# Image pipeline with stages moved between the attention pairs, a second pair of slack, and one residual addition moved from VectorE to GpSimd

## The reference, cut to what matters

```python
block 0:  x = x + _L0_conv_ref(_gn(x), ...)   # 16 images, 128 x 32 x 32, fp32
    shared = silu(group_norm(conv1x1_grouped(x)))            # 8 groups
    two experts of 8, chosen per image by a router:
    expert_out = sum_k rw[k] * silu(group_norm(conv3x3_grouped(x, expert k)))
    return shared + expert_out
block 1:  x = x + _L1_conv_ref(_gn(x), ...)                  # _gn: 32 groups
    qkv = qkv_w @ x + qkv_b;  windows of 8x8 pixels, 8 heads of 16 channels
    attn = softmax(q @ k.T / 4 + bias);  o = attn @ v
    out = proj_w @ (o + depthwise_conv7x7(v)) + proj_b
```

## Time and profile before

| | us |
|---|---|
| median of 3 runs | 931.92 |
| lowest and highest | 928.15, 932.22 |
| the profiled execution | 934.59 |
| its span, first to last instruction | 932.9 |
| its mean granted TensorE clock | 0.879 of full |

### The profile page before, as it was taken

One profiled execution on the slowest core, in us unless ns is written; L12 is line 12 of the kernel. 1 busy time (PEld: TensorE's weight loads), 2 busy tenths in 40 slices (PEclk: granted clock), 3 DMA queues, 4 the chain that ended last, 5 costly groups with the idle time before them and its releaser, 6 DMA issues.

```text
span 932.9 us, 18414 instructions
## 1 busy us (share of the span) xinstructions
PE 743.6 (80%) x6926; PEld 422.7 (45%) x6926; DVE 578.1 (62%) x1136; ACT 457.7 (49%) x746; POOL 197.0 (21%) x289
## 2 busy tenths in 40 slices
PE   6143768888888989888989887979797989978785
PEld 5121334454545554545454545454545456534321
DVE  4724456675767666767676757575757587632296
ACT  1204546555555564646464646464646465344422
POOL 3122123131213140403130313131313020000044
PEclk9976969797979797979888988888988989999999
DMA  9224444545464545455554545454546254586435
GB/s 353 106 71 116 139 113 146 145 128 156 144 178 136 163 148 150 150 153 165 142 170 128 173 136 173 123 173 120 177 132 177 67 176 132 161 276 217 156 157 203
DMA packets 84046, 145.29 MB, mean 156 GB/s; under 512 B 24179, under 2 KB 48886, under 8 KB 83958
## 3 DMA queue, kind: packets, MB, share of 16 engines
q1 hardware_dynamic: 58102, 100.89, 34.8%
q0 software_dynamic: 21248, 25.36, 10.9%
q10 hardware_dynamic: 4608, 17.86, 5.2%
HBM read 84.21 MB, written 51.41 MB: 145 GB/s over the span
## 4 chain that ended last, share of the span: by engine, by line
PE 41%; DMA 19%; DVE 16%; ACT 8%; issue 7%; SPq 6%; POOL 1%; POOLq 1%; ACTq 0%; DVEq 0%
PE g L1061 11%; DMA sk_d<-khl 10%; PE g L1057 5%; PE g L1079 4%; PE t L1127 4%; DMA stack<-sk_d 3%; SPq L298 3%; ACT xw L540 3%; PE s L1116 3%; PE pv L1142 3%; DMA vt<-x 3%; PE t L1241 2%; PE s L1112 2%; SPq L292 2%; PE s L1241 2%
## 5 line engine op out<-in xcount | busy, mean ns | idle before, releaser
L806 DVE BATCH_NORM_STATS2 st<-y 128x6 f32<-128x512 f32 x96 | 66.6, 694 | 147.6 <-ACT y L522 147.6
L522 ACT ACTIVATE y<-g 128x512 f32<-128x512 f32 x96 | 57.2, 596 | 167.0 <-PE g L1061 87.0
L1061 PE MATMUL g<-xsh,wsel 96*128 96x512 f32 x256 | 127.8, 627 | 14.0 <-DMA xsh<-xs 10.5
L595 ACT ACTIVATE pt<-t 128x512 f32<-128x512 f32 x128 | 76.2, 597 | 118.8 <-PE t L1127 112.2
L870 DVE TENSOR_REDUCE mx<-s 128x8 f32<-128x512 f32 x128 | 87.8, 686 | 69.6 <-PE s L1116 69.6
L1127 PE MATMUL t<-ident,less 128*128 128x128 f32 x512 | 97.6, 321 | 3.7 <-DVE less L874 3.7
L1142 PE MATMUL pv<-vp,pt 128*64 128x34 f32 x2048 | 95.2, 242 | 5.0 <-ACT pt L595 4.8
L1112 PE MATMUL s<-bias,ident 128*128 128x512 f16 x128 | 56.7, 443 | 52.9 <-DMA stack<-sk_d 52.8
L1142 PEld LDWEIGHTS pv<-vp,pt 128*64 128x64 f32 x2048 | 80.1, 154 | 31.4 <-issue 25.0
L874 DVE TENSOR_TENSOR less<-s,mx 128x512 f32<-128x512 f32 x128 | 88.5, 692 | 4.4
L1079 PE MATMUL g<-xw,w 128*128 128x512 f32 x128 | 66.7, 640 | 15.4 <-ACT y L522 11.7
(11 more groups left out here) (159 smaller groups left out, 1158.5 us busy)
## 6 DMA issues: line engine op xcount, KB each, us to landing
xsh<-xs POOLq DMA_DIRECT2D x64, 210.0 KB, 5.4
stack<-sq_d SPq DMA_DIRECT2D x96, 128.0 KB, 3.1
stack<-sk_d SPq DMA_DIRECT2D x192, 64.0 KB, 2.8
xs<-xn ACTq DMA_DIRECT2D x16, 578.0 KB, 2.9
vt<-x SPq DMA_DIRECT2D x4, 2048.0 KB, 17.7
xin<-x POOLq DMA_DIRECT2D x16, 512.0 KB, 5.8
acc_d<-xr SPq DMA_DIRECT2D x16, 512.0 KB, 5.5
sq_d<-qhl SPq DMA_DIRECT2D x16, 512.0 KB, 7.7
```

The costliest lines, as they stand in the source:

```text
L522: act.activation(y[:, k, h * HALF:(h + 1) * HALF], g[h][:, :], ACT.Identity).then_inc(g_free[h], 1)
L595: act.activation(pt[:, p % 2].rearrange("p i w n -> p (i w n)"), tbk[p % 2][:, :], ACT.Exp).then_inc(sem["exp_done"], 1)
L806: last = v.bn_stats(st[:, 2 * k + h, :], y[:, k, h * HALF:(h + 1) * HALF])
L1061: last = mm(g[h][:, :], wsel[:, k - 1, C * dy:C * dy + C], xsh[:, k - 1, dy + 16 * h:dy + 16 * h + 16, 0:W], start=(dy == 0), stop=(dy == 1))
```

## The change

The stages are put in other pairs, PE gets scores two pairs ahead, `pt` gets a third place, the halves of q and k are saved each by itself, the `g` banks are used in one alternating order for both halves, and `residual` part 0 becomes `add_input` on POOL, between `choose_affine` and the `rsqrt` of x; `split_v` stays last in POOL's turn and its DMAs are issued by SP in the turn after. No arithmetic changes. The waits on `g_ready` and `g_free` take their bank and count from the new order (`wait_ready`, `wait_emptied`).

```diff
     for b in range(B + 1):
+        use("y2", b + 2, (0,))
+        use("q", b + 1, (0,))
+        use("y2", b + 2, (1,))
+        use("q", b + 1, (1,))
+        use("k", b + 1)
+        use("v", b + 1)
+        use("ot", b - 1, (1,))
+        use("pr", b - 1)
+        use("vt", b + 1)
+        use("y0", b + 3)
+        use("y1", b + 3)
+        use("ot", b, (0,))
+    return {key: (n % 2, n // 2) for n, key in enumerate(order)}
...
-        pt = sb("pt", [C, 2, Q, 2, TOK])
+        pt = sb("pt", [C, 3, Q, 2, TOK])
...
+            def save_half(j, half, name, dst, src, saved):
+                cols = slice(HALF * half, HALF * half + HALF)
+                wait_emptied(sp, name, j, half)
+                if j:
+                    sp.wait_ge(stacked[half], STACK * j)
+                sp.dma_start(dst.rearrange("t c n -> c t n")[:, :, cols], src[:, :, cols]).then_inc(saved[half], 16)
...
             def step(b, has1, has2, has3):
+                if b:
+                    load_x1(b - 1)
                 place_v(b)
                 if has1:
                     save_q(b + 1)
                     save_k(b + 1)
-                    stack_qk(b + 1, 0)
+                    stack_q(b + 1, 0)
+                    stack_k(b + 1, 0)
                 if b:
                     save_acc(b - 1)
-                load_x1(b)
                 if has1:
-                    stack_qk(b + 1, 1)
+                    stack_q(b + 1, 1)
+                    stack_k(b + 1, 1)
                 if has2:
                     save_xr(b + 2)
...
+            def add_input(j):
+                pool.wait_ge(sem["silu_done"], 3 * j + 1)
+                if j:
+                    pool.wait_ge(sem["xr_saved"], 16 * j)
+                    pool.wait_ge(sem["xw_done"], j)
+                nc.gpsimd.tensor_tensor(xr[:, :], y[:, 0, :], xin[:, j % 2, :], ALU.add).then_inc(sem["sum_shared"], 1)
...
             def step(b, has1, has2, has3):
                 if has3:
-                    load_x(b + 3)
-                if has1:
-                    rsqrt(b + 1, 1, 1)
-                if has3:
                     load_rows(b + 3)
                 if has2:
                     rsqrt(b + 2, 0, 3)
                 if has3:
                     choose_affine(b + 3)
+                if has2:
+                    add_input(b + 2)
+                if b + 4 < B:
+                    load_x(b + 4)
+                if has2:
+                    rsqrt(b + 2, 1, 1)
                 if has1:
                     split_v(b + 1)
```

More of the change, by code:

```diff
@@ L357, in _ @@
             save_k(0)
-            stack_qk(0, 0)
-            stack_qk(0, 1)
+            for half in range(2):
+                stack_q(0, half)
+                stack_k(0, half)
             save_xr(1)
             images(step)
+            for c in range(TAP_RING):
+                load_taps(c)
+            load_x1(B - 1)
             save_acc(B - 1)
@@ L467, in _ @@
             choose_affine(2)
+            add_input(1)
+            load_x(3)
+            rsqrt(1, 1, 1)
             images(step)
@@ L574, in vt_out @@
                                                   ACT.Identity)
-                    last.then_inc(g_free[h], 1)
+                    last.then_inc(g_free[at], 1)
             def turn_out(b, h):
[L579 to L582, removed]
+                at = wait_ready(act, "ot", b, h)
+                if b:
+                    wait_ready(act, "pr", b - 1, h)
                 for n in range(2):
@@ L648, in _ @@
                 silu(1, k)
+            copy_y(2, 0)
+            window(1)
+            copy_y(2, 1)
             images(step)
@@ L951, in step @@
-                    if p == 5 and has2:
-                        y_coefs(b + 2)
-                    if p == 6:
+                    if has2 and p == 7:
+                        x_coefs(b + 2)
+                    if has1 or p < PAIRS - 2:
+                        maxima(b + (p + 2) // PAIRS, (p + 2) % PAIRS)
+                    if p == 1 and b:
+                        outputs(b - 1, ROWS - 1)
+                    elif p % 2 and p > 1:
+                        outputs(b, p // 2 - 1)
+                    if p < 2:
+                        if has2:
+                            y_stats(b + 2, 2, (p,))
+                        if has1:
+                            low_qk(b + 1, 0, p)
@@ L954, in step @@
+                    if p == 2 and has1:
+                        low_qk(b + 1, 1, 0)
+                        low_qk(b + 1, 1, 1)
+                    if p == 3 and has2:
+                        y_coefs(b + 2)
+                    if p == 4:
+                        if b:
+                            add_projection(b - 1, 0)
+                            add_projection(b - 1, 1)
                         if has1:
                             turn_v(b + 1)
+                    if p == 5 and has2:
+                        for part in range(1, 3):
+                            residual(b + 2, part)
```

453 lines of the change are left out of this document (206 added, 247 removed).

## The result

The changed kernel takes 878.71 us (median of 4 runs, 873.84 to 881.38), the kernel before 932.07; the ratio is 0.943, 95% interval 0.938 to 0.948. The profiled execution is the fastest of the four, 873.84, with a span of 871.8. The forecast was 858 with a range of 828 to 908: faster, as said, and 21 us short of it.

What follows compares the result with a forecast made beforehand. PE, slowed by a low clock and waits, was taken as the bound. Start 148, thirteen turns 524, then 30.5, 16, 18.5 and 122.6 gave a span of 859.6 us, hence 858; range 828 to 908.

Steps and rivals of the forecast that it cites:

- the prediction's own signs: Wrong if turns show 10 us low stretches, scores still wait 3 us for a DMA, or PE waits for banks.
- PE's work: PE's own work in one turn at full clock: 34.5 us, with eight pairs at 1.82 us each.
- The clock: Behind pair 6's 3.5 us wait the clock is low for 3.4 to 6.8 us, losing 2.1 us a turn.
- What bounds now: In the kernel before, PE is nearest to full; each turn pays about 4 us of stack wait plus half of 10 for clock.
- Stacking: Stack's first half lands 10.4 to 13.7 us after pair 3 begins; pair 6's wait falls from 3.7 to at most 1.3.
- Rival C: The stack lands late as saves, row loads and stacking meet: 49.4 us a turn, 977 us in total; chance 0.06.
- DVE in pairs 4 and 5: DVE's chain ends 17.3 us after pair 3 begins, so PE waits 3.5 us for the second average in pair 6.
- The addition on POOL: First residual addition takes 2.37 us on POOL, from 7.8 to 10.2, hidden by 2.5 us of cover, at no cost.
- SBUF port: POOL and DVE's two-SBUF-operand additions exclude each other; split of v up to 2.1 us late, within 3 in hand: no cost.
- Rival B: Low clock stretch stays as long, or unseen waits cost as much: 5.1 to 6.8 us a turn, 897 to 919; chance 0.2.
- Rival D: No change: the wait only moves, clock and small gaps stay, and a turn remains 45.9 us; chance 0.04.

Runs made afterwards that it cites:

- all four: The changed kernel with the stack's second half, second expert's rows and load of x later, and four unread products ahead of pair 6's scores: 835.4 us, 0.897.

## Why the prediction was right, and where it was not

The forecast of 858 and its range of 828 to 908 hold 878.7, and faster was right. By the prediction's own signs the mechanism did less well: it was to be wrong if the scores still waited 3 us for a DMA or if turns showed low stretches of 10 us, and both happened. From pair 3 to pair 3 the second to the thirteenth turn take 41.5 us in the mean for 40.3, because two errors offset each other in part. The second average comes at 19.8 us in the mean for 17.4, which is 2.4 too late. PE's work behind it takes 19.7 at full clock for 20.8, which is 1.1 too little. The clock adds 2.0 to that where 2.1 was taken. With the 20.8 of the prediction the total would be some 14 us higher. That the number lies as near as it does is luck in part.

*What bounds now.* Right: the wait for the stack and the clock behind it are what the experiments move.

*PE's work* was put too high, 34.5 us. With the unread products PE is busy for 438.6 us in twelve turns at a clock of 0.99, that is 36.5 a turn, 32.8 without the products' 3.7. The term at fault is the pair: 1.82 was read from the order of before, and the new one takes 1.57.

*Stacking.* This is the step that failed. It let the first half land at 10.4 to 13.7 after pair 3 begins, "usually near 2.3" after its last issue. In the turn shown it lands at 19.3. The half save took 7.5, inside the 5 to 8 taken, but the readers 8.3 behind the last issue, where the earlier trace rows had 5.8 as the longest. The row was read as what one such transfer takes. It is what it takes in stretches in which 0.5 to 0.8 of the engines are busy; the change moved transfers together until 0.96 were. The clue stood in the rows: a stretch of the same turn with a DMA share of 0.95 in the earlier trace rows, and the k save's 2.8 to 8.9.

*Rival C* had the mechanism, and a time (20.4) that the worst turn reaches (20.2) and the mean (17.8) does not; its price was wrong: 49.4 us a turn against 41.5. It also had the kernel slower than before from a landing of about 17 on, and at 17.8 it is 5.7% faster. It charged 6.8 us for the clock. Of the low stretch of the turn shown, 455.7 to 465.9, 3.0 us lie in the wait itself, where nothing is lost. In the mean a turn loses 2.0 us behind the second average (21.8 against the 19.7 of the kernel with unread products) and 0.9 from pair 6's scores to it (2.0 against 1.1), 3.0 together.

*DVE in pairs 4 and 5.* Right to 0.5 us, 16.8 for 17.3, and shown as the next bound with the rows left out.

*The addition on POOL.* Its duration (2.38 for 2.37), place (7.6 to 10.0 for 7.8 to 10.2) and cover were right, the zero cost was not. The step named what stands behind the addition on POOL and asked when each was wanted, not what each would collide with: the load of x, released early, cost 14 to 17 us. In the first images the wait was in my walk (128.8 for the second average, 131.1 measured) but put down as the place of the work, with no look at what undoing it would give: 7.6 us ahead of the turns.

*SBUF port.* In the changed kernel POOL's cast beside no DVE addition takes 1.03 us where it took 1.89; this agrees with the reading of the rows, and no cost of it is seen.

*The clock.* The low stretches are 6.8 us in four of the thirteen turns, 10.2 in eight and 13.7 in one, not 3.4 to 6.8. With the rows left out, where the wait is the one that was predicted (3.4 us), they are 3.4 or 6.8, and a turn loses 2.1 behind the average, as said. That the fall comes from the wait, and can be kept away by work in it, the unread products show.

*Rival B* was right in that the low stretches stay as long as they were, and wrong in their price, 5.1 to 6.8 for 3.0. *Rival D*, a turn of 45.9, is ruled out by 41.6. No waits for banks appear in pairs 0 to 2 of the turn shown, and its pairs other than 6 take 3.4 to 4.4 each: pair 5 0.5 over the sum, the others 0.2 to 0.3 under it.

What stays open: how the 14 us divide between x's share of the engines and its order in the queues; why the k save stays at 7.3 us with half of the rows moved and falls to 2.2 with all of them gone; and how many products are best, since only three and four were tried.

## What to carry to other kernels

A transfer's time from the trace holds for the other transfers that ran beside it there. Before stages are moved, add up the bytes that will be in flight between the issue and the use of the critical transfer, and ask of each instruction that gets earlier which load it sets free. A wait of PE that can't be removed may be worth filling with products that nobody reads, ahead of the wait; and what is neutral in a loop can still cost ahead of it.

## What the runs showed of the hardware

More work made PE faster: 3.7 us of unread products in each of 13 turns took the mean granted clock of the turns from 0.89 to 0.98 and 29 us off the total. The same products behind the wait took the gains of all four back (879.8 against 835.4). Waits of PE for the stack of 0.9 to 1.6 us left the clock at 1.0 in that kernel, those of 2.9 to 5.6 did not. Transfers of one size took 2.1 to 9.8 us by what ran beside them: the q half saves and the k half saves have 256 KB each, and landed in 2.2 and in 7.9 at the median in the changed kernel. With the loads of rows left out, which go through POOL's queue and not SP's, the k half saves took 2.2 as well.
